# The last pair's four hops by batch, with the turned probabilities as stationary operand, and four output buffers

## The chip, the cores and the metric

One core of a Trainium2 chip runs the whole kernel. The metric is the device time of one execution in microseconds, the median of several. TensorE (PE in the profile) multiplies, VectorE (DVE), ScalarE (ACT) and GpSimd (POOL) work on tiles, and SyncE (SP) issues the DMAs.

## The reference

64 graphs of 128 nodes with 256 features go through two attention layers with 8 heads of 32. Layer 0 is masked attention with an output projection, a residual and a LayerNorm. Layer 1 is what this case is about:

```python
q = x @ Wq.T + bq; k = x @ Wk.T + bk; v = x @ Wv.T + bv        # split into 8 heads of 32
pros = softmax(where(adj == 0, -16384, q k^T), axis=-1)        # 128x128 for each head
z = v
for _ in range(4):
    z = 0.9 * (pros @ z) + 0.1 * v                             # four hops
y = x + z
out = (y - mean(y)) / sqrt(var(y) + 1e-5) * gamma + beta
```

## The kernel before

The batch is cut into 32 pairs of graphs; a tile holds a pair (two batches b = 0 and 1). Each engine has its own list of steps, written out by hand: `begin()`, a loop `step(t)` in which many pairs are under way at different stages, and `end()`, in which the pipeline drains. An engine runs its list strictly in order, and steps of different engines meet through semaphores. The change touches the end, above all the last pair R = Pair(31), and the pair before it, Q = Pair(30).

Layer 1 of a pair goes so. `scores` (TensorE) writes q k^T into the four banks psS. `mask_scores` (VectorE), `exp_two` (ScalarE), `reciprocals` (VectorE) and `probabilities` (GpSimd, one per batch) make pr, the probabilities. `turn_probs` (L401) turns four heads of a batch on TensorE, and `save_pT` (L1022, ScalarE) copies them to pT1, where for each batch and head a block of 128 x 128 lies with the neighbour m on the partitions. A hop is then `hop` (L411, TensorE, through `spread`), `save_hop` (L1045 on ScalarE or L1416 on VectorE, times 0.9), `turn_hop` (L456, TensorE) and `add_hop` (L1512, VectorE, plus 0.1 v, or in the last hop plus zf, the residual). `spread` takes 32 columns of z as stationary operand (128 x 32) and streams the 128 columns of pT, four heads side by side in the array; what comes out lies with the features on the partitions, which is why each hop needs the eviction to hT and the transposes. Each fp32 product is two pairs of a weight load (LDWEIGHTS) and a MATMUL instruction: 16 products are 32 of each.

LayerNorm 1 is `statistics` (L1450), `aggregate` (L1463) and `add_eps` (L1470) on VectorE, `inverse_root` on GpSimd (L1872, a power of -0.5), then for most pairs `normalise(1, b, p)` (L1482, VectorE) into o_t, `scale_out` (L1921) and `shift_out` (L1927) on GpSimd and `store` (L293, SyncE). The last two pairs end with `finish(b, p)` instead: two VectorE instructions (L1491 and L1495) and a store for each batch (L290).

Three things set the order near the end. There are two output buffers o_t, and normalise(1, b, p) waits until the store of pair p - 2 has landed; what stands behind it in VectorE's list waits too, such as add_hop(3, 29) and save_hop(0, 31). All four hops of pair 31 depend on each other through four engine steps. The fold at the kernel's start (L473, `folds`) is the one place in which whole blocks of 128 x 128 fp32 weights are loaded for products that stream very little: one column.

Of the kernel before, what the change touches and what calls it, by code (L numbers as in the profile page):

```python
# [66 lines left out]
class DmaCount:  # L67
# [3 lines left out]
        self.sems = sems  # L71

    def sem(self, pair):
        return self.sems[pair.parity]

    def at(self, pair):
        return 16 * max(0, pair.number // 2 + 1)


def two_layers(nc, x, x_t, adj, w, rows, cols, ident_d, out):  # L80
    ctx = ExitStack()
    with ctx:
        def sb(name, shape, dt=FP32):
            return ctx.enter_context(nc.sbuf_tensor(name, shape, dt))
# [7 lines left out]
        def sem(name):  # L92
            return ctx.enter_context(nc.semaphore(name))
# [68 lines left out]
        hT = [sb(f"hT{i}", [128, 2 * C, N]) for i in range(2)]  # L162
        z = [sb(f"z{i}", [128, 2, D]) for i in range(2)]
        y1 = [sb(f"y1_{i}", [128, 2, D]) for i in range(2)]
        o_t = [sb(f"o_t{i}", [128, 2, D]) for i in range(2)]

        psS = bank("psS", 4)
        F = [bank(f"psF{i}") for i in range(4)]
# [56 lines left out]
        xt_s = DmaCount([sem("xt_even"), sem("xt_odd")])  # L225
        adj_s = DmaCount([sem("adj_even"), sem("adj_odd")])
        x_s = DmaCount([sem("x_even"), sem("x_odd")])
        st_s = DmaCount([sem("store_even"), sem("store_odd")])

        w_in = [sem(f"w_in{i}") for i in range(NW)]  # L230
        row_in = sem("rows_in")
# [9 lines left out]
        fold_s = sem("folds_saved")  # L241
        scaled_s = [sem(f"last_scaled{b}") for b in range(2)]
        end_s = [sem(f"last_out{b}") for b in range(2)]

        block = ctx.enter_context(nc.Block())

# [17 lines left out]
        def _(sp):  # L264
# [21 lines left out]
            def store(p):  # L286
                if p.last_two:
                    for b in range(2):
                        sp.wait_ge(end_s[b], p.number - Q.number + 1)
                        sp.dma_start(out[p.number * 2 + b], o_t[p.parity][:, b, :]).then_inc(st_s.sem(p), 16)  # L290
                elif p.real:
                    sp.wait_ge(o_s.sem, o_s.at(p))
                    sp.dma_start(out[bass.ds(p.number * 2, 2)].rearrange("b n d -> n b d"), o_t[p.parity][:, :, :]  # L293
                                 ).then_inc(st_s.sem(p), 16)

            load_xt(P0)
# [19 lines left out]
                load_adj(t + 2)  # L316

            run(step, 0, PAIRS + 9)
            for p in (Q, R):
                sp.wait_ge(st_s.sem(p), st_s.at(p) + 16)  # L320

        @block.tensor
        def _(pe):
# [126 lines left out]
            def turn_hop(j, p):  # L450
                if p.real:
                    pe.wait_ge(hT_s[j].sem, hT_s[j].at(p))
                    for b in range(2):
                        for c in range(C):
                            o = b * D + c * 128
                            last = nc.tensor.transpose(ps_u[j][:, o:o + 128], hT[p.parity][:, b * C + c, :], ident[:, :])  # L456
                    last.then_inc(zr[j].sem, 1)

            def folds():

# [273 lines left out]
            def end():  # L734
# [208 lines left out]
                hop(2, Pair(30))  # L943
                free((pT_s[1][1][1], Pair(31)))
                turn_hop(3, Pair(29))
                free((pT_s[1][0][0], Pair(31)))
                hop(0, Pair(31))
                free((hT_s[2], Pair(30)))
                turn_hop(0, Pair(31))
                free((hT_s[0], Pair(31)))  # L950
                turn_hop(2, Pair(30))
                free((z_s[3], Pair(29)))
                hop(1, Pair(31))
                free((z_s[0], Pair(31)))
                hop(3, Pair(30))
                free((z_s[2], Pair(30)))
                turn_hop(1, Pair(31))
                free((hT_s[1], Pair(31)))
                turn_hop(3, Pair(30))
                free((hT_s[3], Pair(30)))  # L960
                hop(2, Pair(31))
                free((z_s[1], Pair(31)))
                turn_hop(2, Pair(31))
                free((hT_s[2], Pair(31)))
                hop(3, Pair(31))
                free((z_s[3], Pair(30)))
                turn_hop(3, Pair(31))

            begin()
            run(step, 7, PAIRS)  # L970
# [3 lines left out]
        def _(act):  # L974
# [235 lines left out]
            def end():  # L1210
# [113 lines left out]
                save_hop(1, Pair(31))  # L1324
                save_hop(3, Pair(30))
                save_hop(2, Pair(31))
                save_hop(3, Pair(31))

            begin()
            run(step, 7, PAIRS)  # L1330
# [3 lines left out]
        def _(dve):  # L1334
# [137 lines left out]
            def normalise(l, b, p):  # L1472
                if p.real and not (l and p.last_two):
                    dve.wait_ge(rstd_s[l].sem, rstd_s[l].at(p))
                    if l:
                        dve.wait_ge(st_s.sem(p), st_s.at(p - 2))
                        y, dst, done = y1[p.parity], o_t[p.parity], on_s[b]
                    else:
                        dve.wait_ge(x1r.sem, x1r.at(p - 2))
                        dve.wait_ge(xg_s.sem, xg_s.at(p - 2))  # L1480
                        y, dst, done = y0, xn[p.parity], xn_s[b]
                    nc.vector.tensor_scalar(dst[:, b, :], y[:, b, :], mv[l][:, b, 0:1], rstd[l][:, b:b + 1],  # L1482
                                            ALU.subtract, ALU.mult).then_inc(done.sem, 1)

            def finish(b, p):

                if p.last_two:
                    n = p.number - Q.number + 1
                    dve.wait_ge(rstd_s[1].sem, rstd_s[1].at(p))
                    dve.wait_ge(st_s.sem(p), st_s.at(p - 2))  # L1490
                    nc.vector.scalar_tensor_tensor(out=o_t[p.parity][:, b, :], in0=y1[p.parity][:, b, :],  # L1491
                                                   scalar=mv[1][:, b, 0:1], in1=row[:, GA1, :],
                                                   op0=ALU.subtract, op1=ALU.mult).then_inc(scaled_s[b], 1)
                    dve.wait_ge(scaled_s[b], n)
                    nc.vector.scalar_tensor_tensor(out=o_t[p.parity][:, b, :], in0=o_t[p.parity][:, b, :],  # L1495
                                                   scalar=rstd[1][:, b:b + 1], in1=row[:, BE1, :],
                                                   op0=ALU.mult, op1=ALU.add).then_inc(end_s[b], 1)

            def add_hop(j, p):
                if p.real:  # L1500
# [6 lines left out]
                    else:  # L1507
                        if j == 0:
# [2 lines left out]
                        dst, add = z[p.parity], z0s[p.parity]  # L1511
                    nc.vector.tensor_tensor(dst[:, :, :], ps_u[j][:, :].rearrange("p (b d) -> p b d", b=2), add[:, :, :],  # L1512
                                            ALU.add).then_inc(z_s[j].sem, 1)

            def save_fold(n):
                dve.wait_ge(fold_r, 3 if n else 1)
# [209 lines left out]
            def end():  # L1726
# [91 lines left out]
                save_hop(0, Pair(31))  # L1818
                statistics(1, Pair(29))
                aggregate(1, Pair(29))  # L1820
                add_hop(0, Pair(31))
                add_hop(2, Pair(30))
                add_eps(1, Pair(29))
                add_hop(1, Pair(31))
                add_hop(3, Pair(30))
                normalise(1, 1, Pair(29))
                normalise(1, 0, Pair(29))
                statistics(1, Pair(30))
                aggregate(1, Pair(30))
                add_hop(2, Pair(31))  # L1830
                add_eps(1, Pair(30))
                normalise(1, 0, Pair(30))
                finish(0, Pair(30))
                normalise(1, 1, Pair(30))
                finish(1, Pair(30))
                add_hop(3, Pair(31))
                statistics(1, Pair(31))
                aggregate(1, Pair(31))
                add_eps(1, Pair(31))
                normalise(1, 1, Pair(31))  # L1840
                finish(1, Pair(31))
                normalise(1, 0, Pair(31))
                finish(0, Pair(31))

            begin()
            run(step, 7, PAIRS)
# [3 lines left out]
        def _(pool):  # L1850
# [66 lines left out]
            def scale_out(p):  # L1917
                if p.real and not p.last_two:
                    for b in range(2):
                        pool.wait_ge(on_s[b].sem, on_s[b].at(p))  # L1920
                    nc.gpsimd.tensor_tensor(o_t[p.parity][:, :, :], o_t[p.parity][:, :, :], both(row[:, GA1:GA1 + 1, :]),  # L1921
                                            ALU.mult).then_inc(og_s.sem, 1)

            def shift_out(p):
                if p.real and not p.last_two:
                    pool.wait_ge(og_s.sem, og_s.at(p))
                    nc.gpsimd.tensor_tensor(o_t[p.parity][:, :, :], o_t[p.parity][:, :, :], both(row[:, BE1:BE1 + 1, :]),  # L1927
                                            ALU.add).then_inc(o_s.sem, 1)

            def begin():  # L1930
                add_bias(Pair(0))
# [64 lines left out]
            def end():  # L1996
# [43 lines left out]
                scale_out(Pair(30))  # L2040
                shift_out(Pair(29))
                inverse_root(1, Pair(31))
                scale_out(Pair(31))
                shift_out(Pair(30))
                shift_out(Pair(31))

            begin()
            run(step, 7, PAIRS)
# [31 lines left out]
```

## Time and profile before

| what | value |
|---|---|
| median of 3 runs | 784.21 us (783.15 to 788.16) |
| span of the profiled execution | 784.0 us |
| TensorE busy / its weight loads | 754.1 us / 710.6 us |
| VectorE, ScalarE, GpSimd busy | 637.1, 665.7, 547.8 us |
| TensorE's clock | 2.4 GHz, but for three stretches (17.5 to 24, 765 to 768.3, and from 778.6 us on) |

The profile is one execution. Its page says how long each engine was busy, and for 40 slices of the span what clock TensorE was granted; 1.00 is 2.4 GHz and 0.50 is 1.2 GHz. A timeline line gives the start, the time until the last of a group of like instructions ended, the engine, the line, the tiles and the count, and in brackets how long the engine had been idle and who ended that.

### The profile page before, as it was taken

What the parts mean: (1) busy time and instruction counts of PE and PEld (TensorE: products, weight loads), DVE (VectorE), ACT (ScalarE), POOL (GpSimd) and SP (SyncE); (2) the same over time, 40 slices, a digit from 0 to 9 for tenths busy, and PEclk for the clock granted to TensorE, in tenths of its full rate; (3) what the DMA queues carried; (4) which work ended last, traced back from release to release, by engine and by line L of the source; (5) the groups of instructions that cost most, each with busy time, mean ns of one, the idle gap of its engine ahead of it and who ended that gap; (6) DMA issues with size and microseconds to landing.
All of it is one profiled execution on the core that took longest, in us unless ns stands there. A gap on an engine that the chain in (4) does not pass through costs nothing.

```text
span 784.0 us, 32528 instructions
## 1 busy us (share of the span) xinstructions
PE 754.1 (96%) x11544; PEld 710.6 (91%) x11544; DVE 637.1 (81%) x3093; ACT 665.7 (85%) x2570; POOL 547.8 (70%) x417
## 2 busy tenths in 40 slices
PE   6889999999999999999999999999999999999974
PEld 6778999999999999999999999999999999998863
DVE  5778888888888888888888888888888888887765
ACT  4779998889889988988998898998889899899661
POOL 0336858666777777777787777787777778768774
PEclk9899999999999999999999999999999999999997
DMA  7101011010111101111111011111001111100002
GB/s 239 48 21 50 23 35 37 22 30 23 50 50 49 50 29 26 47 50 49 50 49 30 23 51 50 49 49 50 29 23 50 50 50 36 30 16 17 29 15 68
DMA packets 33245, 34.12 MB, mean 44 GB/s; under 512 B 2368, under 2 KB 28864, under 8 KB 33088
## 3 DMA queue, kind: packets, MB, share of 16 engines
q1 hardware_dynamic: 33088, 32.06, 13.8%
q8 instruction: 94, 1.54, 0.8%
q14 instruction: 63, 0.52, 0.2%
HBM read 23.67 MB, written 8.39 MB: 41 GB/s over the span
## 4 chain that ended last, share of the span: by engine, by line
PE 89%; DVE 3%; ACT 2%; issue 2%; DMA 1%; SPq 1%; POOL 1%; POOLq 0%; DVEq 0%; ACTq 0%
PE psF L342 23%; PE psF L411 18%; PE psF L351 16%; PE psF L401 15%; PE psS L391 9%; PE psF L456 7%; PE psF L436 2%; ACT ex L1011 2%; DMA w_raw<-in_w 1%; DVE sm L1400 1%; DMA out<-o_t 1%; SPq L284 0%; DVE o_t L1491 0%; DVE bst L1450 0%; POOL o_t L1927 0%
## 5 line engine op out<-in xcount | busy, mean ns | idle before, releaser
L1011 ACT ACTIVATE ex<-sm,nmax 128x128 f32<-128x128 f32 x1024 | 397.9, 397 | 3.3 <-DVE nmax L1400 2.3
L1859 POOL TENSOR_TENSOR pr<-ex,rec 128x1024 f32<-128x1024 f32 x128 | 245.3, 1918 | 101.1 <-DVE rec L1409 101.1
L1400 DVE CUSTOM_DVE_ANT_0 sm<-psS,mask 128x128 f32<-128x128 f32 x1024 | 228.3, 284 | 41.6 <-PE psS L391 41.4
L1011 ACT ACTIVATION_READ_ACCUMULATOR ex<-sm,nmax 128x1 f32 x1024 | 200.7, 196 | 0.0
L1022 ACT ACTIVATE pT<-psF 128x512 f32<-128x512 f32 x256 | 138.8, 596 | 34.5 <-PE psF L401 34.4
L401 PE MATMUL psF<-ident,pr 128*128 128x128 f32 x1024 | 137.8, 276 | 0.8 <-ACT pT L1022 0.5
L401 PEld LDWEIGHTS psF<-ident,pr 128*128 128x128 f32 x1024 | 112.7, 141 | 9.3 <-ACT pT L1022 0.9
L342 PE MATMUL psF<-xh,w_hi 128*128 128x256 f32 x512 | 112.6, 302 | 7.7 <-DVE w_lo L1339 5.7
L411 PE MATMUL psF<-pT,z 128*32 128x128 f32 x3072 | 103.1, 276 | 2.3 <-DVE z L1512 2.0
L342 PE MATMUL psF<-xh,w_lo 128*128 128x256 f32 x512 | 104.1, 285 | 0.0
L342 PE MATMUL psF<-xl,w_hi 128*128 128x256 f32 x512 | 103.6, 284 | 0.0
L342 PEld LDWEIGHTS psF<-xh,w_hi 128*128 128x128 f32 x512 | 79.8, 193 | 14.2 <-issue 12.6
L411 PEld LDWEIGHTS psF<-pT,z 128*32 128x32 f32 x3072 | 84.2, 111 | 8.1 <-issue 3.5
L1880 POOL TENSOR_TENSOR xb<-x_in,bo_row 128x512 f32<-128x512 f32 x32 | 41.7, 1302 | 70.2 <-DVE y L1439 52.9
L1400 DVE DVE_READ_ACCUMULATOR2_ANT nmax<- 128x1 f32 x1024 | 84.8, 83 | 0.0
L456 PE MATMUL psF<-ident,hT 128*128 128x128 f32 x512 | 76.4, 273 | 5.7 <-DVE hT L1416 3.9
L342 PEld LDWEIGHTS psF<-xh,w_lo 128*128 128x128 f32 x512 | 80.5, 193 | 0.0
L342 PEld LDWEIGHTS psF<-xl,w_hi 128*128 128x128 f32 x512 | 80.3, 192 | 0.0
L1872 POOL TENSOR_TENSOR rstd<-ve,mhalf 128x2 f32<-128x2 f32 x64 | 47.2, 737 | 43.5 <-DVE ve L1470 43.3
L391 PE MATMUL psS<-kT,qT 32*128 32x128 f32 x2048 | 75.3, 283 | 0.9 <-DVE nmax L1400 0.9
L391 PEld LDWEIGHTS psS<-kT,qT 32*128 32x128 f32 x2048 | 63.2, 186 | 11.8 <-issue 6.7
L1045 ACT ACTIVATE hT<-psF 128x512 f32<-128x512 f32 x96 | 57.0, 596 | 18.1 <-PE psF L411 18.0
(76 smaller groups left out, 1425.7 us busy)
## 6 DMA issues: line engine op xcount, KB each, us to landing
xt_in<-in_x_t SPq DMA_DIRECT2D x32, 256.0 KB, 3.0
x_in<-in_x SPq DMA_DIRECT2D x32, 256.0 KB, 3.0
out<-o_t SPq DMA_DIRECT2D x30, 256.0 KB, 2.2
adj_in<-in_adj SPq DMA_DIRECT2D x32, 128.0 KB, 2.4
pT<-in_w SPq DMA_DIRECT2D x4, 256.0 KB, 4.0
row<-in_rows SPq DMA_DIRECT2D x1, 768.0 KB, 6.8
w_raw<-in_w SPq DMA_DIRECT2D x3, 256.0 KB, 7.0
out<-o_t SPq DMA_DIRECT2D x4, 128.0 KB, 1.7
```

Of the source, the lines that this page charges most:

```text
L342: last = nc.tensor.matmul(dst[:, c * T:(c + 1) * T], w_p[e][:, i, kc, c * 128:(c + 1) * 128], x_p[a][:, kc, :], start=(n == 0 and kc == 0) ...
L351: last = nc.tensor.matmul(dst[:, b * D:(b + 1) * D], x_p[a](kc), w_p[e][:, i, kc, :], start=(n == 0 and kc == 0), stop=(n == 2 and kc == C ...
L391: last = nc.tensor.matmul(psS[:, o:o + N], qT[l][r, c, b * N:(b + 1) * N], kT[l][r, c, b * N:(b + 1) * N], start=True, stop=True)
L401: last = nc.tensor.transpose(ps_T[l][b][c][:, g * N:(g + 1) * N], pr[l][:, b, G * c + g, :], ident[:, :])
L411: last = nc.tensor.matmul(dst[32 * g:32 * g + 32, o:o + N], src[:, b, h * HD:(h + 1) * HD], p_T[:, b, h, :], start=True, stop=True)
L456: last = nc.tensor.transpose(ps_u[j][:, o:o + 128], hT[p.parity][:, b * C + c, :], ident[:, :])
L1011: e = nc.scalar.activation(ex[l][:, b, h, :], sm[l][:, b, h, :], ACT.Exp, scale=-1.0, bias=nmax[l][:, b, h:h + 1], accum_out=tot[l][:, b, ...
L1022: nc.scalar.activation(pT[l][p.parity][:, b, G * c:G * c + G, :], ps_T[l][b][c][:, :].rearrange("p (g n) -> p g n", g=G), ACT.Copy).then_i ...
L1045: nc.scalar.activation(hT[p.parity][:, :, :], ps_h[j][:, :].rearrange("p (a n) -> p a n", n=N), ACT.Copy, scale=1.0 - ALPHA).then_inc(hT_s ...
L1400: last = nc.vector.tensor_tensor_reduce(sm[l][:, b, h, :], psS[:, o:o + N], mask[p.parity][:, b, :], -1.0, BIG, ALU.add, ALU.min, nmax[l][ ...
L1859: nc.gpsimd.tensor_tensor(pr[l][:, b, :, :], ex[l][:, b, :, :], rec[l][:, b, :].unsqueeze(2).broadcast_to([128, H, N]), ALU.mult).then_inc ...
L1872: nc.gpsimd.tensor_tensor(rstd[l][:, :], ve[l][:, :], mhalf[:, :], ALU.pow).then_inc(rstd_s[l].sem, 1)
```

## The change

Four output buffers and four store semaphores take the place of two, so that normalise(1, b, p) waits for the store of pair p - 4. The hops of pair 31 are made by batch: `last_hop(j, b)` takes the turned probabilities of a head (128 x 128) as stationary operand and streams 32 columns of v or z, so that the result lies as z does, in the psS banks; `take_hop(j, b)` on VectorE scales by 0.9 and adds in one instruction. The four evictions and four rounds of transposes of that pair go. The LayerNorm of pair 31 is made by batch too, with `last_root(b)` on GpSimd, and the first instruction of `finish` no longer waits for the root. The lists at the end are reordered.

```diff
-        return self.sems[pair.parity]
+        return self.sems[pair.number % len(self.sems)]
-        return 16 * max(0, pair.number // 2 + 1)
+        return 16 * max(0, pair.number // len(self.sems) + 1)
-        o_t = [sb(f"o_t{i}", [128, 2, D]) for i in range(2)]
+        o_t = [sb(f"o_t{i}", [128, 2, D]) for i in range(4)]
@@ tensor
+            def last_hop(j, b):
+                if j:
+                    pe.wait_ge(hop_s[b], j)
+                else:
+                    pe.wait_ge(v_s[1].sem, v_s[1].at(R))
+                    for saved in pT_s[1][b]:
+                        pe.wait_ge(saved.sem, saved.at(R))
+                src = z[R.parity] if j else v1[R.parity]
+                for h in range(H):
+                    o = 512 * b + h * HD
+                    last = nc.tensor.matmul(psS[:, o:o + HD], pT1[R.parity][:, b, h, :], src[:, b, h * HD:(h + 1) * HD],
+                                            start=True, stop=True)
+                last.then_inc(hop_r[b], 1)
@@ tensor, end()
                 turn_hop(3, Pair(29))
-                hop(0, Pair(31))
+                last_hop(0, 0)
+                last_hop(0, 1)
-                turn_hop(0, Pair(31))
                 turn_hop(2, Pair(30))
-                hop(1, Pair(31))
+                last_hop(1, 0)
+                last_hop(1, 1)
                 hop(3, Pair(30))
-                turn_hop(1, Pair(31))
+                last_hop(2, 0)
+                last_hop(2, 1)
                 turn_hop(3, Pair(30))
-                hop(2, Pair(31))
-                turn_hop(2, Pair(31))
-                hop(3, Pair(31))
-                turn_hop(3, Pair(31))
+                last_hop(3, 0)
+                last_hop(3, 1)
@@ vector
-                        dve.wait_ge(st_s.sem(p), st_s.at(p - 2))
+                        dve.wait_ge(st_s.sem(p), st_s.at(p - 4))
+            def take_hop(j, b):
+                dve.wait_ge(hop_r[b], j + 1)
+                src = psS[:, 512 * b:512 * b + D]
...
+                nc.vector.scalar_tensor_tensor(out=dst[:, b, :], in0=src, scalar=1.0 - ALPHA, in1=add[:, b, :],
+                                               op0=ALU.mult, op1=ALU.add).then_inc(hop_s[b], 1)
@@ vector, end(), as it is after
                 add_hop(3, Pair(29))
                 take_hop(0, 0)
                 take_hop(0, 1)
                 statistics(1, Pair(29))
                 aggregate(1, Pair(29))
                 add_hop(2, Pair(30))
                 add_eps(1, Pair(29))
                 take_hop(1, 0)
                 take_hop(1, 1)
                 normalise(1, 1, Pair(29))
                 normalise(1, 0, Pair(29))
                 take_hop(2, 0)
                 take_hop(2, 1)
                 add_hop(3, Pair(30))
                 statistics(1, Pair(30))
                 aggregate(1, Pair(30))
                 add_eps(1, Pair(30))
                 finish(0, Pair(30))
                 finish(1, Pair(30))
                 take_hop(3, 0)
                 last_statistics(0)
                 take_hop(3, 1)
                 last_aggregate(0)
                 last_statistics(1)
                 last_eps(0)
                 last_aggregate(1)
                 last_eps(1)
                 finish(0, Pair(31))
                 finish(1, Pair(31))
```

## Rows read from the trace of the kernel before

**Rows 1.** The page: busy time by engine, and the chain that ended last
```profile
PE 754.1 (96%) x11544; PEld 710.6 (91%) x11544; DVE 637.1 (81%) x3093; ACT 665.7 (85%) x2570; POOL 547.8 (70%) x417
PE 89%; DVE 3%; ACT 2%; issue 2%; DMA 1%; SPq 1%; POOL 1%; POOLq 0%; DVEq 0%; ACTq 0%
```
**Rows 2.** Windows of the end: stretch, length, busy by engine, TensorE's clock, DMA share, GB/s
```profile
700.00:745.00 45.00, 42.71 (x728) 38.74 (x729) 35.60 (x164) 35.97 (x135) 35.95 (x29) 1.00 0.08 26
760.00:765.00 5.00, 2.26 (x53) 1.81 (x48) 3.92 (x10) 0.00 (x0) 3.08 (x3) 1.00 0.10 33
776.60:781.40 4.80, 0.00 (x0) 0.00 (x0) 3.72 (x11) 0.00 (x0) 0.70 (x1) 0.71 0.18 60
```
**Rows 3.** Waits of VectorE over the span: total us, times, longest
```profile
DVE o_t L1482 <- DMA out<-o_t: 6.6, 3, 4.4
```
**Rows 4.** Timeline around the two earlier waits for a store
```profile
735.06 0.41 DVE L1482 TENSOR_SCALAR o_t<-y,mv,rstd 128x256 f32<-128x256 f32 x1 [0.67 <-DMA out<-o_t]
735.94 0.63 PE L436 MATMUL psF<-ident,xn 128*128 128x128 f32 x4 [0.43 <-DVE xn L1482]
740.74 0.41 DVE L1482 TENSOR_SCALAR o_t<-y,mv,rstd 128x256 f32<-128x256 f32 x1 [1.56 <-DMA out<-o_t]
742.46 1.08 PE L411 MATMUL psF<-pT,z 128*32 128x128 f32 x32 [0.29 <-DVE qT L1377]
```
**Rows 5.** Timeline around the longest wait for a store
```profile
756.83 0.70 POOL L1872 TENSOR_TENSOR rstd<-ve,mhalf 128x2 f32<-128x2 f32 x1
759.16 0.42 PEld L456 LDWEIGHTS psF<-ident,hT 128*128 128x128 f32 x4 [0.20 <-issue]
759.75 1.08 PE L411 MATMUL psF<-pT,w_raw 128*32 128x128 f32 x32
761.04 0.73 DVE L1482 TENSOR_SCALAR o_t<-y,mv,rstd 128x256 f32<-128x256 f32 x2 [4.40 <-DMA out<-o_t]
763.12 1.06 PE L456 MATMUL psF<-ident,hT 128*128 128x128 f32 x8 [2.29 <-DVE hT L1416]
```
**Rows 6.** Timeline of the third hop of pair 31, and the start of the fourth
```profile
769.67 1.08 PE L411 MATMUL psF<-pT,z 128*32 128x128 f32 x32 [0.23 <-DVE z L1512]
773.05 1.08 PE L411 MATMUL psF<-pT,z 128*32 128x128 f32 x32 [0.88 <-DVE z L1512]
```
**Rows 7.** The fold's weight loads: min/median/max ns, then the timeline at either clock
```profile
L473 PEld LDWEIGHTS psF<-col,w_raw x16: 190/192/333, 15.9 to 17.9; 128*128 128x128 f32 x16
...
16.13 1.20 PEld L473 LDWEIGHTS psF<-col,w_raw 128*128 128x128 f32 x10
17.69 0.55 PEld L473 LDWEIGHTS psF<-col,w_raw 128*128 128x128 f32 x2
18.12 0.55 PEld L342 LDWEIGHTS psF<-xh,w_hi 128*128 128x128 f32 x2
```
**Rows 8.** Windows of TensorE alone: busy, clock, DMA share, GB/s
```profile
14.60:15.10 0.50, 0.00 (x0) 1.00 1.01 338
15.20:17.40 2.20, 2.20 (x17) 1.00 0.43 127
17.60:18.10 0.50, 0.50 (x4) 0.50 0.62 193
18.10:24.00 5.90, 5.90 (x29) 0.50 0.13 46
763.10:764.90 1.80, 1.32 (x19) 1.00 0.00 0
765.00:768.30 3.30, 3.30 (x62) 0.50 0.16 55
```
**Rows 9.** Timeline of the very end, then mean ns of VectorE forms, from the groups by shape
```profile
778.65 0.70 POOL L1872 TENSOR_TENSOR rstd<-ve,mhalf 128x2 f32<-128x2 f32 x1 [3.67 <-DVE ve L1470]
781.34 0.81 SPq L290 DMA_DIRECT2D out<-o_t  x2
L1522 DVE TENSOR_TENSOR r_row<-psF,row 128x256 f32<-128x256 f32 x1 | 0.4, 425 | 0.4 <-PE psF L473 0.4
```

More of the change, by code:

```diff
@@ L227, in two_layers @@
         x_s = DmaCount([sem("x_even"), sem("x_odd")])
-        st_s = DmaCount([sem("store_even"), sem("store_odd")])
+        st_s = DmaCount([sem(f"store{i}") for i in range(4)])
         w_in = [sem(f"w_in{i}") for i in range(NW)]
@@ L243, in two_layers @@
         end_s = [sem(f"last_out{b}") for b in range(2)]
+        hop_r = [sem(f"last_hop{b}_ready") for b in range(2)]
+        hop_s = [sem(f"last_hop{b}_saved") for b in range(2)]
+        bn_b = [sem(f"last_bn{b}_done") for b in range(2)]
+        ag_b = [sem(f"last_aggr{b}_done") for b in range(2)]
+        ve_b = [sem(f"last_var_eps{b}_done") for b in range(2)]
+        rstd_b = [sem(f"last_rstd{b}_done") for b in range(2)]
         block = ctx.enter_context(nc.Block())
@@ L289, in store @@
                         sp.wait_ge(end_s[b], p.number - Q.number + 1)
-                        sp.dma_start(out[p.number * 2 + b], o_t[p.parity][:, b, :]).then_inc(st_s.sem(p), 16)
+                        sp.dma_start(out[p.number * 2 + b], o_t[p.number % 4][:, b, :]).then_inc(st_s.sem(p), 16)
                 elif p.real:
                     sp.wait_ge(o_s.sem, o_s.at(p))
-                    sp.dma_start(out[bass.ds(p.number * 2, 2)].rearrange("b n d -> n b d"), o_t[p.parity][:, :, :]
+                    sp.dma_start(out[bass.ds(p.number * 2, 2)].rearrange("b n d -> n b d"), o_t[p.number % 4][:, :, :]
                                  ).then_inc(st_s.sem(p), 16)
@@ L318, in _ @@
             run(step, 0, PAIRS + 9)
+            for p in (Q - 2, Q - 1):
+                sp.wait_ge(st_s.sem(p), st_s.at(p))
             for p in (Q, R):
@@ L945, in end @@
                 turn_hop(3, Pair(29))
-                free((pT_s[1][0][0], Pair(31)))
-                hop(0, Pair(31))
+                last_hop(0, 0)
+                last_hop(0, 1)
                 free((hT_s[2], Pair(30)))
-                turn_hop(0, Pair(31))
-                free((hT_s[0], Pair(31)))
                 turn_hop(2, Pair(30))
+                last_hop(1, 0)
+                last_hop(1, 1)
                 free((z_s[3], Pair(29)))
-                hop(1, Pair(31))
-                free((z_s[0], Pair(31)))
                 hop(3, Pair(30))
-                free((z_s[2], Pair(30)))
-                turn_hop(1, Pair(31))
-                free((hT_s[1], Pair(31)))
+                last_hop(2, 0)
+                last_hop(2, 1)
+                free((hT_s[3], Pair(30)))
                 turn_hop(3, Pair(30))
-                free((hT_s[3], Pair(30)))
-                hop(2, Pair(31))
-                free((z_s[1], Pair(31)))
-                turn_hop(2, Pair(31))
-                free((hT_s[2], Pair(31)))
-                hop(3, Pair(31))
-                free((z_s[3], Pair(30)))
-                turn_hop(3, Pair(31))
+                last_hop(3, 0)
+                last_hop(3, 1)
             begin()
@@ L1323, in end @@
                 save_hop(2, Pair(30))
-                save_hop(1, Pair(31))
                 save_hop(3, Pair(30))
-                save_hop(2, Pair(31))
-                save_hop(3, Pair(31))
             begin()
@@ L1475, in normalise @@
                     if l:
-                        dve.wait_ge(st_s.sem(p), st_s.at(p - 2))
-                        y, dst, done = y1[p.parity], o_t[p.parity], on_s[b]
+                        dve.wait_ge(st_s.sem(p), st_s.at(p - 4))
+                        y, dst, done = y1[p.parity], o_t[p.number % 4], on_s[b]
                     else:
@@ L1488, in finish @@
                     n = p.number - Q.number + 1
-                    dve.wait_ge(rstd_s[1].sem, rstd_s[1].at(p))
-                    dve.wait_ge(st_s.sem(p), st_s.at(p - 2))
-                    nc.vector.scalar_tensor_tensor(out=o_t[p.parity][:, b, :], in0=y1[p.parity][:, b, :],
+                    dve.wait_ge(*((ag_b[b], 1) if p.is_(R.number) else (ag_s[1].sem, ag_s[1].at(p))))
+                    dve.wait_ge(st_s.sem(p), st_s.at(p - 4))
+                    nc.vector.scalar_tensor_tensor(out=o_t[p.number % 4][:, b, :], in0=y1[p.parity][:, b, :],
                                                    scalar=mv[1][:, b, 0:1], in1=row[:, GA1, :],
@@ L1494, in finish @@
                     dve.wait_ge(scaled_s[b], n)
-                    nc.vector.scalar_tensor_tensor(out=o_t[p.parity][:, b, :], in0=o_t[p.parity][:, b, :],
+                    dve.wait_ge(*((rstd_b[b], 1) if p.is_(R.number) else (rstd_s[1].sem, rstd_s[1].at(p))))
+                    nc.vector.scalar_tensor_tensor(out=o_t[p.number % 4][:, b, :], in0=o_t[p.number % 4][:, b, :],
                                                    scalar=rstd[1][:, b:b + 1], in1=row[:, BE1, :],
@@ L1513, in add_hop, with last_statistics, last_aggregate, last_eps @@
                                             ALU.add).then_inc(z_s[j].sem, 1)
+            def take_hop(j, b):
+                dve.wait_ge(hop_r[b], j + 1)
+                src = psS[:, 512 * b:512 * b + D]
+                if j < NUM_HOP - 1:
+                    if j == 0:
+                        dve.wait_ge(z0_s.sem, z0_s.at(R))
+                        dve.wait_ge(hr[NUM_HOP - 1].sem, hr[NUM_HOP - 1].at(R - 2))
+                    dst, add = z[R.parity], z0s[R.parity]
+                else:
+                    dve.wait_ge(zf_s.sem, zf_s.at(R))
+                    for used in on_s:
+                        dve.wait_ge(used.sem, used.at(R - 2))
+                    dst, add = y1[R.parity], zf[R.number % 4]
+                nc.vector.scalar_tensor_tensor(out=dst[:, b, :], in0=src, scalar=1.0 - ALPHA, in1=add[:, b, :],
+                                               op0=ALU.mult, op1=ALU.add).then_inc(hop_s[b], 1)
+            def last_statistics(b):
+                dve.wait_ge(hop_s[b], NUM_HOP)
+                nc.vector.bn_stats(bst[1][:, b, :], y1[R.parity][:, b, :]).then_inc(bn_b[b], 1)
+            def last_aggregate(b):
+                dve.wait_ge(bn_b[b], 1)
+                dve.wait_ge(end_s[b], 1)
+                nc.vector.bn_aggr(mv[1][:, b, :], bst[1][:, b, :]).then_inc(ag_b[b], 1)
+            def last_eps(b):
+                dve.wait_ge(ag_b[b], 1)
+                dve.wait_ge(rstd_s[1].sem, rstd_s[1].at(Q))
+                nc.vector.tensor_scalar(ve[1][:, b:b + 1], mv[1][:, b, 1:2], LN_EPS, None, ALU.add).then_inc(ve_b[b], 1)
             def save_fold(n):
@@ L1817, in end @@
                 add_hop(3, Pair(29))
-                save_hop(0, Pair(31))
+                take_hop(0, 0)
+                take_hop(0, 1)
                 statistics(1, Pair(29))
                 aggregate(1, Pair(29))
-                add_hop(0, Pair(31))
                 add_hop(2, Pair(30))
                 add_eps(1, Pair(29))
-                add_hop(1, Pair(31))
-                add_hop(3, Pair(30))
+                take_hop(1, 0)
+                take_hop(1, 1)
                 normalise(1, 1, Pair(29))
                 normalise(1, 0, Pair(29))
+                take_hop(2, 0)
+                take_hop(2, 1)
+                add_hop(3, Pair(30))
                 statistics(1, Pair(30))
                 aggregate(1, Pair(30))
-                add_hop(2, Pair(31))
                 add_eps(1, Pair(30))
-                normalise(1, 0, Pair(30))
                 finish(0, Pair(30))
-                normalise(1, 1, Pair(30))
                 finish(1, Pair(30))
[L1836 to L1840, printed above, removed]
+                take_hop(3, 0)
+                last_statistics(0)
+                take_hop(3, 1)
+                last_aggregate(0)
+                last_statistics(1)
+                last_eps(0)
+                last_aggregate(1)
+                last_eps(1)
+                finish(0, Pair(31))
                 finish(1, Pair(31))
-                normalise(1, 0, Pair(31))
-                finish(0, Pair(31))
             begin()
@@ L1920, in scale_out @@
                         pool.wait_ge(on_s[b].sem, on_s[b].at(p))
-                    nc.gpsimd.tensor_tensor(o_t[p.parity][:, :, :], o_t[p.parity][:, :, :], both(row[:, GA1:GA1 + 1, :]),
+                    nc.gpsimd.tensor_tensor(o_t[p.number % 4][:, :, :], o_t[p.number % 4][:, :, :], both(row[:, GA1:GA1 + 1, :]),
                                             ALU.mult).then_inc(og_s.sem, 1)
@@ L1926, in shift_out, with last_root @@
                     pool.wait_ge(og_s.sem, og_s.at(p))
-                    nc.gpsimd.tensor_tensor(o_t[p.parity][:, :, :], o_t[p.parity][:, :, :], both(row[:, BE1:BE1 + 1, :]),
+                    nc.gpsimd.tensor_tensor(o_t[p.number % 4][:, :, :], o_t[p.number % 4][:, :, :], both(row[:, BE1:BE1 + 1, :]),
                                             ALU.add).then_inc(o_s.sem, 1)
+            def last_root(b):
+                pool.wait_ge(ve_b[b], 1)
+                pool.wait_ge(end_s[b], 1)
+                nc.gpsimd.tensor_tensor(rstd[1][:, b:b + 1], ve[1][:, b:b + 1], mhalf[:, b:b + 1], ALU.pow
+                                        ).then_inc(rstd_b[b], 1)
             def begin():
@@ L2039, in end @@
                 inverse_root(1, Pair(30))
-                scale_out(Pair(30))
                 shift_out(Pair(29))
[L2042 to L2045, printed above, removed]
+                last_root(0)
+                last_root(1)
             begin()
```

## The prediction

> **What bounds the kernel now.** I read the page first. TensorE is busy for 96% of the span and carries 89% of the chain that ended last [rows 1]. A windows view then shows where this no longer holds. From 700 to 745 us TensorE is busy for 42.7 of 45 us. From 760 to 765 it is busy for 2.26 of 5, with no engine above 4, and from 776.6 on it does nothing [rows 2]. The end is bound by latency, so the change must be costed along the chain of its last 50 us. The waits view names one thing in it: VectorE stood three times, for 6.6 us in all, on stores that had not landed, the longest time for 4.4 us [rows 3]. The timeline shows what hangs on each. The reader should look at the start times and at the bracket.
>
> **The two earlier store waits.** These are 0.67 us before 735.06 and 1.56 us before 740.74 [rows 4]. Behind the first, TensorE waited 0.43 us for the normalised rows of pair 31. Behind the second, save_q(1, 31) came late, and TensorE started hop(1, 29) at 742.46 after 0.29 us idle. With four buffers both waits go. What is late next: the first frees TensorE by between its own idle 0.43 and VectorE's 0.67, I take 0.6; the second adds roughly the idle 0.29, with sequencing 0.4. Everything from the scores of pair 31 on, its exponentials and its probabilities, so starts 1.0 us earlier (bounds 0.4 and 2.2, the sum of the waits). Nothing before 735 moves.
>
> **The long wait.** VectorE stood from 756.64 to 761.04 in normalise(1, 0, 28), with add_hop(3, 29) and save_hop(0, 31) queued behind, and TensorE idled 2.29 us for that hT [rows 5]. With four buffers the next release is the root of pair 28, on GpSimd at 756.83 + 0.70, so 757.5, or 756.5 with the shift of 1.0. Then two normalise (0.73) and add_hop(3, 29), free by 759.6. The first last_hop of pair 31 needs none of these: it needs its probabilities and its turn on TensorE. hop(0, 31) started at 759.75 [rows 5]; last_hop(0, 0) starts 1.0 us earlier, at 758.7.
>
> **What the new hops cost.** A hop of pair 31 before took 3.38 us from start to start, 769.67 to 773.05: 1.08 on TensorE, then eviction, transposes and the sum [rows 6]. The new one is 16 products with a full 128 x 128 block of weights and 32 streamed columns. The trace has no such product. The nearest is the fold: whole fp32 blocks, one column streamed. Ten loads took 1.20 us to the end of the last; with the median 0.19 for one, nine intervals take 1.01, so 0.112 us each at 2.4 GHz. At 1.2 GHz two loads lead from 17.69 to 18.12, so 0.215 each [rows 7]. The other bound is a load that isn't covered by the product before: 32 columns in two passes, a quarter of the transposes' 128 columns, which come every 0.11 us (four loads in 0.42) [rows 5]. That adds 0.027, so 0.14. Since the transposes' own 128-column loads hide behind their products at 0.11, I take 0.112. One last_hop is 16 x 0.112 = 1.79 us, and both batches 3.58: more than the 3.38 that the whole hop took before, evictions included. The gain of the direct form is eaten by weight loads. take_hop is 0.43, as the other sum of 256 columns from PSUM [rows 9], and lies beside the other batch's products. So TensorE is never idle, and it is the bound: 8 x 1.79 = 14.3, two turn_hop of pair 30 at 0.43, one hop(3, 30) at 1.0, sum 16.2. At 2.4 GHz throughout it ends at 758.7 + 16.2 = 774.9, where the last transposes ended at 775.6 before.
>
> **The tail.** At 2.4 GHz VectorE is behind by then. The list that ended pair 31 before (the sum, two statistics, two aggregates, an epsilon, four finish instructions) was 3.72 us busy in 11 instructions [rows 2]. Pair 30's is the same, and its root comes 0.8 after the epsilon [rows 9], of which a first finish instruction now covers some 0.5: from turn_hop(3, 30), ended at 771.3, VectorE is through with pair 30 at 771.3 + 3.72 + 0.5 = 775.5. Pair 31's list loses the sum of 0.69 and gains two take_hop of 0.43 and a second epsilon of 0.17: 4.07 busy, and 0.6 of gaps for 13 instructions, so 780.2. The last result before was ready at 781.34, and the span ended 2.66 later at 784.0 [rows 9]. So 782.9: a gain of only 1.1 us at full clock. Pair 31's root is hidden by VectorE's own list. Where TensorE ends later, VectorE has done pair 30 and the first take_hop and statistics of pair 31 (0.85): from TensorE's end there remain 0.17 for the result, 4.67 - 0.85 = 3.8, and 2.66, so 6.6 us.
>
> **The clock.** This decides. In the fold TensorE was busy for 2.20 of 2.20 us from 15.2 to 17.4, first with 256-column products and from 15.9 [rows 7] with loads and one-column products; yet the clock fell to 1.2 GHz at about 17.5, 1.6 us into these, after 0.5 us of idle at 14.6 [rows 8]. The other fall, at 765, came 4.1 us after TensorE had stopped at 760.8 (759.75 + 1.08) [rows 5], with 1.3 us of work between [rows 8]. So loading weights did not keep the clock up in the fold. The last hops are the same kind of stream: a full load every 0.11 us, and columns for about a quarter of that time. They run for 14.3 us, with the two short transposes and the hop between. I expect the fall 1.6 to 6 us after 758.7, and take 4.1, the other row's: 762.8. It comes back in the rows only after long dense streams, 6 us from 18.1 and 3.3 us from 765 [rows 8]; the only dense piece here, hop(3, 30), is 2 us at the low clock. So it stays low to the end. TensorE's remaining 774.9 - 762.8 = 12.1 us take x 1.93 (0.215 / 0.112, and 2 for the rest), 23.4, and it ends at 786.2. With 6.6 the span ends at 792.8. The median stands 0.2 above the profiled span, so 793.0.
>
> The Trainium skill (page "TensorE: Matmul & The Clock Gate", section "HAM oscillation — how this bites in real kernels") ties a fall of the clock to TensorE standing idle while it waits for data. By that rule alone this stream, which has no idle time, would keep 2.4 GHz, and the sum would be 782.9. The fold's row speaks against it.
>
> **Rivals.**
> - A, the clock holds (chance 0.2). This is the other side: it ends at 783.1, no slower than before. For it: 32 columns a load are more than the fold's one, and the fold had idle time just before. Against it: the fall at 17.5 under full issue. It decides from a fall later than about 773: each us at the low clock costs one us, less the 1.5 that VectorE lags behind. This is also what the skill's rule above would give.
> - B, the product isn't hidden behind the next load (0.07). 128 intervals of 0.14 instead of 0.112 add 3.6 at the high clock and up to 5.5 with the fall: 786.7 to 798.
> - C, the clock falls and returns once, or falls late (0.13). A return after hop(3, 30) that lasts as long as the low stretch of the rows, 3.3 us, gives 789.7; a fall only at 766 gives the same.
> - D, the load of a block is much cheaper than in the fold, for instance because both instructions of a product take the same weights (0.03): TensorE would end some 6 us earlier, VectorE's list would bound, near 777.
> The forecast (fall in the first third, no return) has the rest, 0.57. Its own range follows from the fall: at 760.5 the time is 795.2, at 764.8 it is 791.1.
>
> **How the numbers follow.** Bound of a change that a measurement can tell: 1%, so 776.4 and 792.1. The forecast lies above 792.1 for falls before 763.7, some three quarters of 0.57, so 0.43; B adds 0.04. Slower 0.47. Faster is D alone and a part of it, 0.02. The rest, 0.51, is within 1%. The range takes in A, since forecast and C hold only 0.7: from 782.5 to 796.0.
>
> **What would show it.** Right: weight loads of the new hops 0.11 apart, then 0.215 apart once the clock is 0.50; no wait of VectorE on a store; last_hop(0, 0) near 758.7; TensorE without idle from there to its end; a clock of 0.50 from about 763. Wrong: a clock of 1.00 in that stretch (then 783), loads 0.14 apart, or VectorE waiting somewhere new between 735 and 758, for instance for a root of GpSimd, which would eat the 1.0 us of the shift. Most of all the forecast hangs on the time of the fall, which the trace of before can't tell.

## The result, and the profile after

| | before | after |
|---|---|---|
| median | 783.68 us (6 runs by now) | 790.52 us (6 runs, 790.17 to 790.84) |
| ratio, 95% interval | | 1.0082 (1.0058 to 1.0106) |
| span of the profiled execution | 784.0 us | 788.7 us |

The changed kernel is 0.8% slower. These are the lines of its page: busy time by engine, then the chain that ended last by engine and line (L478 is the product of `last_hop`), and TensorE's clock over 40 slices.

```profile
PE 767.2 (97%) x11528; PEld 725.5 (92%) x11528; DVE 637.9 (81%) x3097; ACT 663.8 (84%) x2567; POOL 549.2 (70%) x418
PE 92%; ACT 4%; DVE 2%; issue 1%; DMA 0%; SPq 0%; DVEq 0%; ACTq 0%
PE psF L350 23%; PE psF L419 18%; PE psF L359 16%; PE psF L409 15%; PE psS L399 9%; PE psF L464 7%; PE psS L478 3%; ACT ex L1026 2%; PE psF L444 2%; ACT pT L1037 0%; DMA pT<-in_w 0%; DVE sm L1412 0%; DVE w_lo L1355 0%; ACT w_hi L997 0%; DVE hT L1428 0%
PEclk9999999999999999999999999999999999999975
```

TensorE has 16 MATMUL fewer than before [rows 1] and is busy for 13 us more. The direct hops of one pair of 32 (L478) hold 3% of the chain. The timeline of the end of the changed kernel: start, time until the last of the group ended, engine, line, what was made, and in brackets the idle time before it and who ended that.

```profile
756.18 3.65 PEld L478 LDWEIGHTS psS<-w_raw,pT 128*128 128x128 f32 x32
760.14 6.61 PEld L478 LDWEIGHTS psS<-z,pT 128*128 128x128 f32 x32
766.82 1.94 PE L419 MATMUL psF<-pT,z 128*32 128x128 f32 x32
768.68 6.90 PEld L478 LDWEIGHTS psS<-z,pT 128*128 128x128 f32 x32 [0.38 <-issue]
776.21 6.95 PEld L478 LDWEIGHTS psS<-z,pT 128*128 128x128 f32 x32
783.33 0.42 DVE L1542 SCALAR_TENSOR_TENSOR y<-psS,zf 128x256 f32<-128x256 f32 x1 [0.53 <-PE psS L478]
785.99 0.48 DVE L1508 SCALAR_TENSOR_TENSOR o_t<-o_t,rstd,row 128x256 f32<-128x256 f32 x1
```

Read the second column. The same 32 loads (both batches of one hop) take 3.65 us in the first hop, 6.6 in the second and 6.9 in the third and fourth. Windows of TensorE alone (stretch, length, busy and count, clock, DMA share, GB/s) say why:

```profile
756.20:760.60 4.40, 4.40 (x43) 0.99 0.19 63
760.80:783.20 22.40, 22.40 (x129) 0.50 0.14 46
```

TensorE was never idle in these stretches, and it ran at 1.2 GHz from 760.5 to the end of its work at 783.29. From VectorE's list of waits the stores are gone, which stood there with 6.6 us before [rows 3]. The largest wait in the end of the kernel is now one for TensorE's direct hops (total, times, longest):

```profile
DVE z L1542 <- PE psS L478: 14.0, 6, 4.3
DVE o_t L1494 <- POOL rstd L1918: 0.9, 1, 0.9
DVE o_t L1508 <- POOL rstd L1918: 0.7, 1, 0.7
```

**Where the time came from.** The two profiled executions differ at their start, though the change touches nothing there: that of before had the clock at 0.50 from 17.5 to 24 us [rows 8], that of after did not. So I measure the end from one event that both have, the residual sum of pair 31 in layer 0 (y from psF and xb, 128 x 512), ahead of everything that the change moves. Before, then after:

```profile
730.42 0.69 DVE L1439 TENSOR_TENSOR y<-psF,xb 128x512 f32<-128x512 f32 x1
...
780.83 0.48 DVE L1495 SCALAR_TENSOR_TENSOR o_t<-o_t,rstd,row 128x256 f32<-128x256 f32 x1
```
```profile
727.99 0.69 DVE L1451 TENSOR_TENSOR y<-psF,xb 128x512 f32<-128x512 f32 x1
...
785.99 0.48 DVE L1508 SCALAR_TENSOR_TENSOR o_t<-o_t,rstd,row 128x256 f32<-128x256 f32 x1
```

From that event to the start of the last instruction there are 50.41 us before and 58.00 after: 7.59 more. The last stores then end 0.46 sooner (788.7 - 786.47 = 2.23, for 784.0 - 781.31 = 2.69), which leaves 7.1; the medians differ by 6.8. I call this time the tail below: 50.4 before, 58.0 after.

### The profile page after: what moved, and what is told of

Same layout as the page of the kernel before. It is cut to its first block, busy times and chain, and to the rows that moved or that the text cites. A ratio compares the mean times of both kernels' runs of the same rounds, so it can differ in the third digit from the quotient of the medians.

```text
span 788.7 us, 32500 instructions
## 1 busy us (share of the span) xinstructions
PE 767.2 (97%) x11528; PEld 725.5 (92%) x11528; DVE 637.9 (81%) x3097; ACT 663.8 (84%) x2567; POOL 549.2 (70%) x418
## 4 chain that ended last, share of the span: by engine, by line
PE 92%; ACT 4%; DVE 2%; issue 1%; DMA 0%; SPq 0%; DVEq 0%; ACTq 0%
PE psF L350 23%; PE psF L419 18%; PE psF L359 16%; PE psF L409 15%; PE psS L399 9%; PE psF L464 7%; PE psS L478 3%; ACT ex L1026 2%; PE psF L444 2%; ACT pT L1037 0%; DMA pT<-in_w 0%; DVE sm L1412 0%; DVE w_lo L1355 0%; ACT w_hi L997 0%; DVE hT L1428 0%
## 5 line engine op out<-in xcount | busy, mean ns | idle before, releaser
L419 PE MATMUL psF<-pT,z 128*32 128x128 f32 x2976 | 99.4, 275 | 0.5 <-DVE z L1525 0.4
L419 PEld LDWEIGHTS psF<-pT,z 128*32 128x32 f32 x2976 | 81.1, 110 | 5.5 <-issue 1.3
L464 PE MATMUL psF<-ident,hT 128*128 128x128 f32 x496 | 74.3, 274 | 1.5 <-DVE hT L1428 1.3
L1060 ACT ACTIVATE hT<-psF 128x512 f32<-128x512 f32 x93 | 55.1, 595 | 17.5 <-PE psF L419 17.3
```

Of the source, the lines that this page charges most:

```text
L419: last = nc.tensor.matmul(dst[32 * g:32 * g + 32, o:o + N], src[:, b, h * HD:(h + 1) * HD], p_T[:, b, h, :], start=True, stop=True)
L1060: nc.scalar.activation(hT[p.parity][:, :, :], ps_h[j][:, :].rearrange("p (a n) -> p a n", n=N), ACT.Copy, scale=1.0 - ALPHA).then_inc(hT_s ...
```

## The experiments

The theory: the direct hops make TensorE the bound of the tail, since each product loads a whole block of weights twice (0.11 us each time) for 32 columns; and under this stream the clock falls, which nearly doubles the time of a load. Rivals: the clock falls for some other reason (idle time, the reordered lists), a load and its product don't overlap, or the buffers were no gain. In the diffs, `...` stands for further lines.

### Four buffers alone, and the direct hops with two

These take the change apart. The first is the kernel before with four buffers, four store semaphores and the wait for the store of pair p - 4:

```diff
-        return self.sems[pair.parity]
+        return self.sems[pair.number % len(self.sems)]
...
-        o_t = [sb(f"o_t{i}", [128, 2, D]) for i in range(2)]
+        o_t = [sb(f"o_t{i}", [128, 2, D]) for i in range(4)]
...
-                        dve.wait_ge(st_s.sem(p), st_s.at(p - 2))
+                        dve.wait_ge(st_s.sem(p), st_s.at(p - 4))
```

> The kernel before with four output buffers alone; hops and lists as before. If the store waits were on the path: the 1.1 us before the scores of pair 31 go, hop(0, 31) to turn_hop(0, 31) closes up by 2.3 to 3 us, and the low stretch of the clock after that idle time (3.3 us at half speed, worth 1.7) may go: 783.7 less 3.4 to 6, so 778 to 780. Rival, something else releases VectorE as late (GpSimd's root or list): 782 to 784.

Measured: 780.79 us, ratio 0.9966 (0.9945 to 0.9987), faster. Timeline around the place of the long wait:

```profile
756.89 0.70 POOL L1874 TENSOR_TENSOR rstd<-ve,mhalf 128x2 f32<-128x2 f32 x1
757.63 1.68 DVE L1484 TENSOR_SCALAR o_t<-y,mv,rstd 128x256 f32<-128x256 f32 x2 [0.93 <-POOL rstd L1874]
759.81 1.08 PE L413 MATMUL psF<-pT,w_raw 128*32 128x128 f32 x32
761.79 1.06 PE L458 MATMUL psF<-ident,hT 128*128 128x128 f32 x8 [0.91 <-DVE hT L1418]
```

The 4.40 us on a store became 0.93 on the root of GpSimd, as the prediction named it. TensorE waits 0.91 for the turn where it waited 2.29 [rows 5], and the low stretch at 765 isn't there: the profile shows 1.00 up to 775.5. The tail is 46.5, 3.9 less than before:

```profile
731.41 0.69 DVE L1441 TENSOR_TENSOR y<-psF,xb 128x512 f32<-128x512 f32 x1
...
777.88 0.48 DVE L1497 SCALAR_TENSOR_TENSOR o_t<-o_t,rstd,row 128x256 f32<-128x256 f32 x1
```

In the median 3.2 us of this are seen. The time is 0.8 above the upper end of what was expected (780).

The other is the changed kernel with two buffers and the wait for pair p - 2 again.

> The changed kernel with two output buffers again; the direct hops stay. If TensorE is the bound through the last hops, VectorE's long wait for a store is hidden behind the first two last_hop and only the 1.1 us before the scores come back: 791.6. Rival, the 4.4 us are all on the path here too: 794 to 795.

Measured: 792.65 us, ratio 1.0106 (1.0066 to 1.0146), and the tail is 60.0, 2.0 more than with four. Its timeline:

```profile
728.38 0.69 DVE L1449 TENSOR_TENSOR y<-psF,xb 128x512 f32<-128x512 f32 x1
...
757.64 3.92 PEld L476 LDWEIGHTS psS<-w_raw,pT 128*128 128x128 f32 x32
759.13 0.73 DVE L1492 TENSOR_SCALAR o_t<-y,mv,rstd 128x256 f32<-128x256 f32 x2 [4.40 <-DMA out<-o_t]
762.17 6.95 PEld L476 LDWEIGHTS psS<-z,pT 128*128 128x128 f32 x32
...
788.37 0.48 DVE L1506 SCALAR_TENSOR_TENSOR o_t<-o_t,rstd,row 128x256 f32<-128x256 f32 x1
```

The wait of 4.40 is back and costs TensorE nothing, as the loads of the first hop run through it. What comes back is the 1.1 us ahead of the scores: the first direct hop starts 29.26 after the common event and not 28.19. That is the theory's 791.6; the other 0.9, which it lacked, goes with the clock, which fell at 760.96 here, 3.3 us into the hops and not 4.3. So the two parts of the change pull in opposite directions, and the same four buffers are worth 3.9 us of tail with the old hops and 2.0 with the direct ones.

### The same loads with more columns behind each

The changed kernel, with each product's 32 columns streamed several times into the free part of psS. Loads, order and waits stay; `take_hop` reads the first 32 columns of each 128.

```diff
-                    o = 512 * b + h * HD
-                    last = nc.tensor.matmul(psS[:, o:o + HD], pT1[R.parity][:, b, h, :], src[:, b, h * HD:(h + 1) * HD],
+                    o = 1024 * b + h * 128
+                    last = nc.tensor.matmul(psS[:, o:o + 4 * HD], pT1[R.parity][:, b, h, :],
+                                            src[:, b, h * HD:(h + 1) * HD].unsqueeze(1).broadcast_to([128, 4, HD]),
...
```

> The changed kernel, but each product of the last hops streams its 32 columns four times (128 columns, into the free part of the psS banks); the first 32 are used. The weight loads are the same. If the clock fell because the array streamed little, it stays at 2.4 GHz, loads stay 0.11 us apart since 128 columns fit behind a load, and the 22.5 us at the low clock shrink by 11.3, of which VectorE's own list gives back about 1.2: 780 to 781. Rival, the loads or their order make the clock fall: 790.5 with a clock of 0.50. Rival, the longer products add to the loads: 0.2 apart at the high clock, 792.

> As the one with 128 columns, but the 32 columns streamed twice (64). The theory of streamed columns gives one of two: 780 to 781 with the clock held, or 790.5 with it fallen; in between if it falls late. The rivals give what they give for 128.

Measured: 782.48 us with 128 columns, ratio 0.9969 (0.9946 to 0.9992), and 782.51 with 64, ratio 0.9982 (0.9966 to 0.9997). Four times the streaming makes the changed kernel 8 us faster. Timeline and window (the window with all engines: PE, PEld, DVE, ACT, POOL, then the clock) of the one with 128:

```profile
727.79 0.69 DVE L1452 TENSOR_TENSOR y<-psF,xb 128x512 f32<-128x512 f32 x1
...
755.97 3.65 PEld L478 LDWEIGHTS psS<-w_raw,pT 128*128 128x128 f32 x32
768.77 3.65 PEld L478 LDWEIGHTS psS<-z,pT 128*128 128x128 f32 x32
777.78 0.48 DVE L1509 SCALAR_TENSOR_TENSOR o_t<-o_t,rstd,row 128x256 f32<-128x256 f32 x1
756.00:772.60 16.60, 16.60 (x171) 16.10 (x169) 8.36 (x23) 0.92 (x2) 9.46 (x9) 1.00 0.15 49
```
The last round of loads and the window with 64 columns:
```profile
769.77 3.65 PEld L478 LDWEIGHTS psS<-z,pT 128*128 128x128 f32 x32
756.80:773.60 16.80, 16.76 (x173) 1.00 0.15 49
```

All four rounds of loads take 3.65 us: the loads stay 0.11 us apart with 64 or 128 columns behind them, as with 32 ahead of the fall, so product and load overlap in full, and the clock is 1.00 throughout. TensorE's idle time ahead of the stream is the same too. Windows of it alone, the changed kernel and then the one with 128 columns:

```profile
747.00:755.00 8.00, 6.20 (x117) 1.00 0.01 2
747.00:755.00 8.00, 6.19 (x117) 1.00 0.01 2
```

Other executions agree: over their whole span all six of the changed kernel have a mean clock of 0.981 or 0.982, and the twenty with 64 or 128 columns 0.990 to 0.998. The number of streamed columns differs from the changed kernel, and with it only where the results lie in psS and how VectorE reads them. So it is the streaming, and not idle time, order or loads, that decides the clock here. What lies between 32 and 64 columns wasn't run. The kernel with 128 also gives the price of the direct hops at full clock: a tail of 50.0 for 128 columns (777.78 - 727.79) against the 46.5 of the old hops with four buffers. They lose 3.5 us even so, and the kernel with the old hops doesn't even have the LayerNorm by batch. The time is some 2 us above the 780 to 781 that was expected: TensorE ends 10.5 us sooner after the common event (44.8 for 55.3), but VectorE, now behind with pair 30, ends 5.7 us after it (778.26 for 772.6) where it was 3.2, and gives back 2.5 and not 1.2.

### The fold at the start

The prediction took its evidence on the clock from the fold, where one column is streamed behind each load. Here the kernel before has 64 instead:

```diff
-                            last = nc.tensor.matmul(ps_fold[:, o:o + 1], raw(i)[:, kc, c * 128:(c + 1) * 128],
-                                                    col[:, BE0c, kc:kc + 1], start=(kc == 0), stop=(kc == C - 1))
+                            last = nc.tensor.matmul(ps_fold[:, o:o + 64], raw(i)[:, kc, c * 128:(c + 1) * 128],
+                                                    col[:, BE0c, kc:kc + 1].broadcast_to([128, 64]), start=(kc == 0), stop=(kc == C - 1))
...
```

> The kernel before; only the fold at the start streams its one column 64 times instead of once, with the same 16 weight loads. It is the same kind of stream as the direct hops, in another place. If little streaming is what lets the clock fall there, the low stretch that began at 17.5 us in the kernel before isn't there in the profile, and the executions that had it gain up to 3.3 us (781 to 783 in the median). Rival, the idle time before the fold (0.5 us at 14.6) makes it fall: the stretch is still there and the time is 783.7.

Measured: 782.88 us, ratio 0.9992 (0.9983 to 1.0002), no difference clear of the noise. Its profile has no low stretch at the start. But this alone doesn't confirm the theory there: the changed kernel with its one-column fold had none either.

```profile
15.63 1.84 PE L496 MATMUL psF<-col,w_raw 128*128 128x1 f32 x16
17.34 0.48 PE L350 MATMUL psF<-xh,w_hi 128*128 128x256 f32 x2
17.66 0.40 PE L350 MATMUL psF<-xh,w_lo 128*128 128x256 f32 x2
```

The products after it come 0.12 us apart, which is the full clock. And the last kernel below, with the 64-column fold, had a long low stretch that began before its fold, after TensorE had waited 1.89 us for a weight to arrive:

```profile
15.60 2.08 PE L472 MATMUL psF<-w_raw,spread_col 128*128 128x256 f32 x4 [1.89 <-DMA w_raw<-in_w]
17.47 2.88 PE L480 MATMUL psF<-col,w_raw 128*128 128x64 f32 x13
15.40:26.00 10.60, 10.40 (x45) 0.52 0.19 61
```

So whether the clock falls near the fold differs from one execution to another. Idle time doesn't sort them. Of the seven profiles with a one-column fold, four fell at 17.4 to 17.8 us (before, four buffers alone, 64 columns in the hops, and the first kernel of the next section), after TensorE had waited 0.60, 1.23, 0.16 and 0.49 us for a weight to arrive ahead of the fold. The three that didn't fall had waited 0.50, 1.43 and 1.29. The columns seem to count, by the mean clocks of whole executions: of 45 of the kernel before, 20 have 0.992 or less, and of the ten with only the fold changed none has (0.993 or 0.994). But they aren't all of it. With one column in the fold and 128 in the hops only one of ten fell so low (0.990, the others 0.997 or 0.998), and with 64 in the fold, in the last kernel below, two of ten (0.991, the others the same). What else makes the clock fall there stays open.

### A version that keeps the good part

Four buffers and the old hops, with what is left of the change: the sum of the last hop and the LayerNorm of pair 31 by batch, and for pair 30 the two halves of `finish` taken apart.

```diff
...
-                finish(0, Pair(30))
...
-                finish(1, Pair(30))
-                add_hop(3, Pair(31))
-                statistics(1, Pair(31))
+                scale(0, Pair(30))
+                scale(1, Pair(30))
+                shift(0, Pair(30))
+                shift(1, Pair(30))
+                last_add(0)
+                last_statistics(0)
+                last_add(1)
+                last_aggregate(0)
+                last_statistics(1)
...
```

> Four output buffers, hops of pair 31 as before the change (32-column weights, evictions and transposes), the sum of its last hop and its LayerNorm by batch as in the changed kernel, and for pair 30 the first instruction of finish ahead of the wait for the root. The last hop's sum no longer waits 1.0 us behind pair 30's finish, and the LayerNorm is 0.7 shorter: 780.8 less 1.7, so 779.1. Rival, only one of them: 780.

Measured: 778.58 us, ratio 0.9952 (0.9926 to 0.9979). With the 64-column fold added:

> The one before with the 64-column fold as well. If both hold they add: 777 to 779, with no low stretch of the clock ahead of the last microseconds. Rival: the fold's stretch is only moved, 779 to 781.

Measured: 777.88 us, ratio 0.9934 (0.9914 to 0.9955). The intervals of the two overlap, so what the fold adds can't be told from nothing. Eight of the ten executions took 777.4 to 778.2 us, as expected. The two others took 782.0 and 782.6, and the first of these is the profiled one, with the low stretch at the start that wasn't expected. VectorE in the first of the two:

```profile
728.98 0.69 DVE L1446 TENSOR_TENSOR y<-psF,xb 128x512 f32<-128x512 f32 x1
...
768.61 1.80 DVE L1502 SCALAR_TENSOR_TENSOR o_t<-o_t,rstd,row 128x256 f32<-128x256 f32 x2 [0.26 <-POOL rstd L1905]
770.34 0.41 DVE L1511 TENSOR_TENSOR y<-psF,zf 128x256 f32<-128x256 f32 x1
773.78 0.48 DVE L1502 SCALAR_TENSOR_TENSOR o_t<-o_t,rstd,row 128x256 f32<-128x256 f32 x1
```

The tail is 44.8, 1.7 less than with four buffers alone, as expected: the wait for the root is 0.26 (it was 0.81 and 0.82 with four buffers alone), and the last hop's sum no longer stands behind pair 30. Both kernels are faster than before and than the change.

## Why the prediction was right

The forecast was 793.0 us by a fall of the clock, its range 782.5 to 796.0; measured are 790.5, 0.8% above before. That is inside the 1% to which the prediction gave 0.51, against 0.47 for slower. On the profiled spans it was 792.8 - 784.0 = 8.8 us more, and behind the common event 7.1 came. By its steps:

- **What bounds.** Right. The tail was bound by latency, and after the change TensorE is the bound from 756.2 to 783.3 without idle time.
- **The two earlier store waits.** Taken at 1.0 us. last_hop(0, 0) starts 28.19 after the common event, where hop(0, 31) started 29.33 after it [rows 5]: 1.14.
- **The long wait.** Right: no store holds VectorE there, the root of pair 28 releases it (after 0.94 us), and the first last_hop doesn't hang on it, which the kernel with two buffers shows.
- **What the new hops cost.** Right: 0.112 us for each load, 3.58 for both batches by the sum, and measured 3.65 to the end of the last load. At 1.2 GHz the sum said 0.215, and 32 loads took 6.95, or 0.213 apart with 0.33 for the last.
- **The tail at full clock.** The sum said 1.1 us less than before. The kernel with 128 columns has 0.4 less on the tail and 0.46 in the store, 0.9 in all.
- **The clock.** The fall and its lasting to the end are right. Taken 4.1 us into the hops, it came after 4.3 (760.5), which makes 0.2 us less. This closeness is luck: the 4.1 was the delay of another fall, one after idle time [rows 8], and the kernel with two buffers fell after 3.3. TensorE's work at the low clock then took 0.2 less than the sum had.
- **From TensorE's end to the last result.** Taken as 0.17 + 3.8, measured 3.2 (783.29 to 786.47), 0.8 less: in the timeline the short instructions of the two batches overlap by up to 0.1 us each, where I had added gaps. The stores took 2.23, not 2.66, so 0.4 less.

These terms (0.1, 0.2, 0.2, 0.8, 0.4) are the 1.7 by which the 8.8 was too high. One more step was weak, and by luck cost little: the median was put 0.2 above the profiled span. In the changed kernel an execution of 790.57 us has a span of 788.7, so 1.9 lie outside, and the forecast was 1.7 too low by it. The profiled execution of before was one of the slower ones (40 of the 45 later executions have a shorter span): it reached the common event 2.4 us later than the changed kernel (730.42 - 727.99), with the low stretch from 17.5 us on its way, and the forecast was that much too high. The two errors nearly cancel: 0.7 remain, and with the 1.7 of the terms they are the 2.5 by which 793.0 was too high, to 0.1. The evidence for the clock was weaker than it read, too: an identical copy of the fold ran through at full clock in the changed kernel. What the forecast needed, that few columns behind each load let the clock fall, is shown by the kernels with 64 and 128 columns, not by the fold.

Of the rivals, A (the clock holds, 783.1) is what the 128-column kernel did, at 782.5, so its price was near and only its condition was missing. The rule of the Trainium skill (page "TensorE: Matmul & The Clock Gate", section "HAM oscillation — how this bites in real kernels"), a fall through idle time, would have given that for the change too; the windows show a fall after 4.3 us without any idle time, and the same 1.8 us of idle time ahead of them in a kernel that didn't fall. B (loads 0.14 apart) and D (cheap loads) fell with the 3.65 us. C did not happen: the 1.94 us of hop(3, 30) brought no return. Two small slips of the sums change nothing: C's two cases come to 789.9 and 790.0 by its own terms and not 789.7, and the 3.72 us of VectorE's list in 11 instructions hold 0.1 of an instruction of pair 30, as the list has ten.

## What to carry to other kernels

A product whose result lies right saves the eviction and the transposes, but it is priced by its stationary operand: here each product of 32 columns loaded a 128 x 128 fp32 block twice, 0.11 us each time, and a hop of 3.6 us of loads replaced a chain of 3.4. Look also at the granted clock of such a stream, and not only at its busy share: here it halved although the engine was 100% busy. Streaming the same columns two or four times behind the loads added nothing to their 3.65 us and kept the clock, so it is worth a run. When a change bundles parts, run each alone: the buffers alone gained 3.2 us, and what was added to them lost 9.7 (790.52 for 780.79).

## What the runs showed of the hardware

- TensorE at 100% busy in the profile, with loads of 128 x 128 and 32 streamed columns, fell to 1.2 GHz after 3.3 and 4.3 us in the two profiles with it, and stayed there for the rest of the stream, 22.8 us in the changed kernel. With 64 or 128 columns and the same loads it held 2.4 GHz for the whole stream, windows of 16.8 and 16.6 us.
- A 128 x 128 fp32 load hides a 128-column fp32 product wholly: 32 loads took 3.65 us with 32, 64 or 128 columns.
- The same fold, with the same instructions, ran at 0.50 after 17.5 us in one profiled execution and at 1.00 in another, and the first was 2.4 us behind at the event that both have, which no edit explains. A single profiled execution should be compared from an event that lies behind such a stretch.
